# Low half of each weight: one 128x2048 GpSimd operation or two of 128x1024 with a product between them

## What is computed

```python
xn = _layernorm(x, axis=-1)
s = _ssm(xn, ...)          # conv, silu, delta = softplus(...), then over time, for 512 channels x 16 states:
#   a = exp(delta * A);  b = delta * B_in * x_conv;  h = a_t * h + b_t;  y = sum_n h * C_in + x * D_param
g = _silu(_ffn(xn, ...))   # top 2 of 8 experts, capacity 1024 tokens each:
#   h = gelu(disp @ fc1_w + fc1_b);  eo = h @ fc2_w + fc2_b;  y += gate * eo[...]
out = x + s * g
```

## Time and profile before

| | us |
|---|---|
| median of 3 runs (lowest to highest) | 2114.82 (2114.29 to 2119.66) |
| the profiled execution | 2111.89 |
| its span, from the first to the last instruction | 2110.1 |
| front part, up to the main loop | about 285 |
| main loop | about 285 to 2000 |
| tail | about 110 |

### The profile page before, as it was taken

How to read it: one execution, slowest core, us unless ns; L and a number is a source line. 1 busy time by engine, 2 the same in 40 slices (tenths; PEclk the granted TensorE clock), 3 DMA queues, 4 the chain that set the end, 5 groups by cost and what they waited for, 6 DMA issues and landing times. The chain is left out here.

```text
span 2110.1 us, 30181 instructions
## 1 busy us (share of the span) xinstructions
PE 1883.4 (89%) x9032; PEld 1463.7 (69%) x9032; DVE 1823.3 (86%) x1959; ACT 1230.0 (58%) x1799; POOL 1314.4 (62%) x581
## 2 busy tenths in 40 slices
PE   6599839999999999999999999999999999999900
PEld 3233227888788788878788778887887788778800
DVE  6556549989998999888988998899889988998869
ACT  3268746566655665656566655665566656565433
POOL 1167758566856685668566856786578657766600
PEclk9799959999999999999999999999999999999955
DMA  8714364123522351135114421442144223522199
GB/s 286 257 41 122 82 222 94 65 70 130 120 65 70 131 121 63 65 137 116 66 61 144 100 81 60 145 96 85 60 142 99 78 67 125 116 68 73 34 303 380
DMA packets 88548, 244.78 MB, mean 116 GB/s; under 512 B 13169, under 2 KB 14193, under 8 KB 77169
## 3 DMA queue, kind: packets, MB, share of 16 engines
q1 hardware_dynamic: 70640, 207.30, 28.5%
q0 software_dynamic: 17536, 35.73, 9.3%
q10 hardware_dynamic: 256, 0.26, 0.1%
HBM read 171.56 MB, written 71.70 MB: 115 GB/s over the span
## 5 line engine op out<-in xcount | busy, mean ns | idle before, releaser
L1016 POOL TENSOR_TENSOR ub_sb<-u_sb,brow_sb 128x1024 f32<-128x1024 f32 x256 | 640.4, 2502 | 418.9 <-DVE a_sb L1106 416.1
L1106 DVE TENSOR_TENSOR_SCAN a_sb<-a_sb,state,ub_sb 128x512 f32<-128x512 f32 x512 | 885.4, 1768 | 10.5 <-issue 6.3
L772 PE MATMUL pm<-xTh,w1l 128*128 128x512 f32 x1024 | 423.7, 414 | 9.2 <-issue 5.0
L772 PE MATMUL pm<-w2h,hl 128*128 128x512 f32 x1024 | 423.9, 414 | 0.0
L774 PE MATMUL pm<-w2h,hh 128*128 128x512 f32 x1024 | 402.6, 393 | 0.0
L774 PE MATMUL pm<-xTh,w1h 128*128 128x512 f32 x1024 | 402.1, 393 | 0.0
L773 PE MATMUL pm<-w2l,hh 128*128 128x512 f32 x1024 | 399.4, 390 | 0.0
L773 PE MATMUL pm<-xTl,w1h 128*128 128x512 f32 x1024 | 398.6, 389 | 0.0
L1077 DVE SCALAR_TENSOR_TENSOR s_acc<-pt,ct_keep,s_acc 128x512 f32<-128x512 f32 x480 | 351.7, 734 | 23.4 <-PE pt L802 22.6
L920 ACT ACTIVATE a_sb<-delta_sb,neg_a_keep 128x512 f32<-128x512 f32 x512 | 330.1, 713 | 6.7
L802 PE MATMUL pt<-m_ident,a_sb 128*128 128x128 f32 x2048 | 307.8, 273 | 24.2 <-DVE a_sb L1106 16.7
(11 more groups left out here) (135 smaller groups left out, 1986.6 us busy)
## 6 DMA issues: line engine op xcount, KB each, us to landing
w_raw<-in_w SPq DMA_DIRECT2D x64, 1024.0 KB, 5.0
brow_sb<-b_chunks SPq DMA_DIRECT2D x128, 256.0 KB, 3.5
moe_rows<-zeros_sb SPq DMA_DIRECT2D x5, 2048.0 KB, 16.7
xin_sb<-in_x SPq DMA_DIRECT2D x8, 1024.0 KB, 6.3
xn_rows<-xn_sb SPq DMA_DIRECT2D x8, 1024.0 KB, 8.4
delta_chunks<-ln_sb SPq DMA_DIRECT2D x8, 1024.0 KB, 5.2
u_chunks<-u_now_sb SPq DMA_DIRECT2D x16, 512.0 KB, 4.9
delta_sb<-delta_chunks SPq DMA_DIRECT2D x8, 1024.0 KB, 8.2
```

The lines of the kernel that those rows point to most:

```text
L772: pe.matmul(out, sl, mh, start=start, stop=False)
L1016: pool.tensor_tensor(ub[:, h], u[:, 2 * h:2 * h + 2, :], brow[:, m % 2:m % 2 + 1, :].to_broadcast([P, 2, CH]), ALU.mult).then_inc(s_["bmul ...
L1106: op = dve.tensor_tensor_scan(abuf[:, m, 2 * h + k, :], abuf[:, m, 2 * h + k, :], ub[:, h, k, :], state[:, ds(col, 1)], ALU.mult, ALU.add)
```

## The change

The low half of each weight is computed in two operations of 128x1024, over the first and the last two of the four K blocks. One product for the scans stands between them: for `w1` the first half is ahead of product 0 and the second behind it; for `w2` the first is behind product 2 and the second behind product 3. Only the second raises `w_lo`, so that everyone who waits for a low half waits for both. No other engine's program changes.

```diff
+            LOWS = {0: (0, 1), 2: (1, 0), 3: (1, 1)}
...
-                    def low(which):
+                    def low(which, part):
                         hi, lo = ((w1h, w1l), (w2h, w2l))[which]
                         pool.wait_ge(s_["w_hi"], 2 * it + which + 2)
-                        pool.tensor_tensor(lo[:].rearrange("p k f -> p (k f)"), raw[:], hi[:].rearrange("p k f -> p (k f)").bitcast(F32), ALU.subtract).then_inc(s_["w_lo"], 1)
-
-                    low(0)
+                        w = raw[:].rearrange("p (k f) -> p k f", k=KT)
+                        k = slice(KT // 2 * part, KT // 2 * (part + 1))
+                        op = pool.tensor_tensor(lo[:, k], w[:, k], hi[:, k].bitcast(F32), ALU.subtract)
+                        if part == 1:
+                            op.then_inc(s_["w_lo"], 1)
+
+                    low(0, 0)
...
-                        if i == 2:
-                            low(1)
+                        if i in LOWS:
+                            low(*LOWS[i])
```

## The result

| | before | changed |
|---|---|---|
| median of 6 runs each (us) | 2114.45 | 2093.9 |
| lowest to highest | 2111.15 to 2119.66 | 2092.08 to 2095.55 |
| span of the profiled execution | 2110.1 | 2092.1 |

The ratio is 0.9902, with a 95% interval from 0.9889 to 0.9914: faster by 20.6 us. Forecast were 2107 us and a range from 2096 to 2119.

What follows compares the result with a forecast made beforehand. TensorE was taken to bound the main loop, with 32 us idle there. The terms, 7 x (-0.9 - 0.5) + 2.4 - 0.3 = -7.7 us, led to 2107.1 us, with a range from 2096 to 2119.

Steps and rivals of the forecast that it cites:

- What excludes what, and for how long: Scans and GpSimd operations exclude each other, one instruction at a time, first in line goes; a half takes 2.41 us.
- The turn: Turn of a chunk, 7 times: scan pair ends 2.1 us earlier, the wait for `s_acc` goes; -0.9 us each.
- the 1.07 us: TensorE's wait for `s_acc` at the turn of a chunk, forecast to go: -1.07 us.
- the 0.2 us that I deducted for the cut: Two halves at 2.41 us cost 0.2 us more than the whole `w1` low half at 4.62.
- The second quarter: New wait of 1.0 us at layer 1, scan waits of 0.40 and 1.12 go: -0.5 us, counted 7 times.
- Chunk 0: Layer 1 starts 2.4 us later with product 0 in between, 0.3 us comes back in the second quarter.
- the 3.33 us wait: TensorE's wait at 338.54 in chunk 0, forecast to stay and not to hide the 2.4 us.
- The sum: 7 x (-0.9 - 0.5) + 2.4 - 0.3 = -7.7 us on the profiled span of 2110.1.
- No change: Rival, 2115 us: in the second quarter the exclusion's order turns, `w1l` is 1.15 us later, nothing is left; chance 0.30.
- The dear half: Rival, 2120 us, slower: a half costs 2.80 us, 0.4 us more each; chance 0.14.
- All waits go: Rival, 2096 us: layer 1 is not held up in the second quarter, -19 us; chance 0.09.

Runs made afterwards that it cites:

- no_product_between: Changed kernel with the halves of both weights back to back, no product between; 2107.48 us, where the kernel before took 2120.32.
- w2_cut: Changed kernel with only the low half of `w2` cut, that of `w1` whole; 2106.95 us, where the kernel before took 2120.32.
- lows_set: Changed kernel with memsets in place of the low-half subtractions, but for each half's first 64 columns; 2096.34 us, where the kernel before took 2120.64.
- w1_cut: Changed kernel with only the low half of `w1` cut, that of `w2` whole; 2110.94 us, where the kernel before took 2120.32.
- chunk0_whole: Changed kernel with the low half of `w1` whole in the first quarter of chunk 0; 2099.43 us, where the kernel before took 2121.93.
- changed_again: The changed kernel run again, unedited; 2101.40 us, where the kernel before took 2121.93.
- middle_pair: Changed kernel with the halves of `w1` back to back, ahead of product 0, in the two middle quarters; 2091.86 us, where the kernel before took 2121.93.
- half_b_twice: Changed kernel with one more 128x1024 subtraction ahead of the second half of `w1` in the middle quarters; 2137.78 us, ratio 1.0076 to the kernel before.

## Why the prediction was wrong, point by point

- **What excludes what, and for how long: right where the change needs it.** The pair at the turn became 2.2 us shorter (forecast 2.1), and a half is 2.40 us (2.41). That the exclusion goes from one instruction to the next in line is not so everywhere: in `no_product_between` a waiting scan was held through two halves at 9 of 45 places.
- **The turn, forecast 7 x (-0.9): measured 387.4 - 400.6, 7 x (-1.9).** This is the step that failed by its size: the mechanism was right, and the term came out at half of what the turn gave. First, I took the 1.07 us from the matmul's row; the turns at chunks 0 and 6, which have no other wait, became 1.45 us shorter (55.96 to 54.50). The 0.2 us that I deducted for the cut don't show there either. The weight load of the same step shows the wait in full (before, at the turn to chunk 3):

```profile
943.12 0.42 PEld L802 LDWEIGHTS pt<-m_ident,a_sb 128*128 128x128 f32 x4 [1.49 <-DVE s_acc L1077]
```

  Second, in the five turns inside the chunk loop the idle time at layer 1 fell too, from 1.4 to 1.7 us to 0.6 to 1.15. I hadn't looked at that row. It is worth 3 us in sum, and why it fell stays open. The view of waits names `part` for some of these turns, but the `part` whose bank layer 1 takes had ended 7 us before layer 1 started in both kernels (942.40 against 949.74 before, 935.15 against 942.65 in the changed one). In the three kernels that hold the pair at the turn in full (before, `w2_cut`, `no_product_between`) this time is 1.4 to 2.0 us; in the others it is 0.6 to 1.2, but in `lows_set`, where the pair comes earliest, 2.1 to 2.3. So an earlier pair alone doesn't shorten it.
- **The second quarter, forecast 7 x (-0.5).** Layer 1's new wait for `w1l`, forecast 1.0, is 0.69 by its row and 0.93 by its weight load. The waits of 0.40 and 1.12 went, as forecast, and were worth 1.98 us by the quarter (52.98 to 51.00), not 1.52. First and second quarters of chunks 1 to 7 together: 731.9 to 726.5, or 7 x (-0.8). In it is a new wait for a scan in the first quarters, 0.2 to 0.7 us, that I hadn't forecast.
- **What a wait costs.** A wait of TensorE costs more than the idle time ahead of its matmul says: 1.45 us for 1.07 at the turn, 1.98 for 0.40 and 1.12 together, and 0.92 for 0.65 where it stands alone in the second quarters of `w1_cut` (51.91 us against 50.99). That is 0.2 to 0.4 us for each wait.
- **Chunk 0, forecast +2.1: measured -1.4** (first `w1l` to layer 1 of the second quarter 61.45 to 60.5, the second quarter 51.5 to 51.0). This is the step that had the wrong sign. I had put the 2.4 us of the product onto everything behind it, as if TensorE set the pace there; `chunk0_whole` shows that they are absorbed. And I had kept the 3.33 us wait, which is gone. Counted from the first `w1l`, TensorE starts 2.4 us later (7.07 against 4.71), and product 3 ends 2.2 us sooner (28.6 against 30.8), since only one half of `w2l` stands ahead of it; half B then holds the pair for 1.1 us, not for 2.4. What bounds the stretch now is the new 2.27 us wait for `w1l`: in `w2_cut`, which has neither wait, it takes 57.2 us. Changed kernel, GpSimd and VectorE:

```profile
330.10 3.00 POOL L1021 TENSOR_TENSOR ub_sb<-u_sb,brow_sb 128x1024 f32<-128x1024 f32 x1
332.63 2.82 POOL L1008 TENSOR_TENSOR w2l<-w_raw,w2h 128x1024 fp32r<-128x1024 f32 x1
...
334.18 3.54 DVE L1111 TENSOR_TENSOR_SCAN a_sb<-a_sb,state,ub_sb 128x512 f32<-128x512 f32 x2
```

  With the wait went a stretch at half clock, in the kernel before, from 339 to 342 us:

```profile
339.00:342.00 3.00, 3.00 (x10) 2.44 (x9) 3.00 (x5) 0.00 (x0) 2.70 (x3) 0.50 1.11 217
```

- **The sum.** By the trace, -13.2 for the turns, -5.5 for first and second quarters, -1.4 for chunk 0: -20.1 us against -7.7. Of the 12.4 us between, 6.9 are the turns, 2.0 the second quarters and 3.5 chunk 0.
- **Rivals.** "No change" needed a scan to get in ahead of half B in the second quarter, or half A to come behind both scans of its pair. In the profiled execution neither happened: half A (986.25) stands between the two scans, and half B (992.48) goes 0.1 us ahead of the pair (992.58). The margins were as small as feared: in chunk 7 of `changed_again` half A comes behind both scans, and layer 1 waits 1.66 us instead of 0.7. The dear half isn't one (2.40 us). "All waits go" came nearest in time, and not in mechanism: layer 1 does wait in every second quarter, 7.2 us in all, and `middle_pair`, where it doesn't, is faster still. The range was too narrow below, since its lower end was made of idle times ahead of matmuls, without the 0.2 to 0.4 us that each wait costs more, and without the idle time at layer 1 in the turns.

## What to carry to other kernels

Where two engines exclude each other, don't count how long they hold each other in sum; look for the few hold-ups that the bounding engine waits for, and cut or move the instruction there and only there. A cut pays when the piece fits into the other engine's gap, and costs when the last piece is what the bounding engine wants. For a wait of TensorE don't take the idle time ahead of the matmul as its price; look at the weight load's row too (1.49 us for a wait worth 1.45, 1.54 and 0.82 for two worth 1.98), and see whether the clock behind it was at half. And look whether the semaphore that a view names for a wait could have been the last one.

## What the runs showed of the hardware

- `tensor_tensor_scan` is held by a GpSimd operation that reads SBUF, for up to its whole length, and not by memsets (2.50 us for a pair beside three of GpSimd's instructions, two of them memsets; 4.5 beside a 2.40 us subtraction). Between two such operations in a row a waiting scan got in at 36 of 45 places of `no_product_between` and at 16 of 16 in the middle quarters of `middle_pair`; at the other 9 it was held through both, for 5.7 us at a turn.
- After 2.1 to 2.3 us idle at the turns of `lows_set` and 3.9 us in `half_b_twice` TensorE was granted half its clock, 1.2 GHz, for some us, at a cost of 1.6 us each (2.4 in three quarters of `half_b_twice`). After 2.63 us idle in `chunk0_whole` it was not. So the length of the wait alone doesn't tell; what else does stays open:

```profile
372.00:376.00 4.00, 4.00 (x20) 3.35 (x21) 4.00 (x6) 3.97 (x7) 2.39 (x1) 1.00 0.79 258
```

- What TensorE waits for at layer 1 in the turns inside the chunk loop isn't settled, in `lows_set` (2.3 us) as in the kernels before (1.4 to 1.7) and after (0.6 to 1.15). In `lows_set` `w1l` and the `part` of its bank were there by 942 us by their rows, 7 us before layer 1's start, and the one token tile that came later (948.88 to 949.57) ended after layer 1's start; the turns of chunks 0 and 6, which don't go round the chunk loop, have no such wait.
